# k by token from the DMA queue instead of TensorE in a fused linear-attention kernel, with state copies on GpSimd and other orders at both ends

## The reference, cut to what matters

```python
x = x + attn(layernorm(x), W_attn, b_attn, W_proj, b_proj)
x = x + ffn(layernorm(x), weight, bias)

# attn: 16 heads of 32; q, k = elu(.) + 1; v as it is
kv   = kv + k_t (outer) v_t        # running state, over the tokens of a sequence
ksum = ksum + k_t
y_t  = (q_t @ kv) / (q_t @ ksum + 1e-6)
attn = y @ W_proj + b_proj

# ffn: x and weight clipped to +-448 and rounded to float8_e4m3fn
ffn  = fp8(x) @ fp8(weight).T + bias
```

## Time and profile before

| what | us |
|---|---|
| runs of the kernel before | 987.88, 989.68, 990.79 |
| time of the profiled execution | 989.57 |
| its span, first to last instruction | 987.8 |
| TensorE busy in it | 951.9 |
| ScalarE busy | 743.6 |
| VectorE busy | 703.1 |
| GpSimd busy | 503.9 |

### The profile page before, as it was taken

One profiled execution on the slowest core, in us unless ns is written; L12 is line 12 of the kernel. 1 busy time (PEld: TensorE's weight loads), 2 busy tenths in 40 slices (PEclk: granted clock), 3 DMA queues, 4 the chain that ended last, 5 costly groups with the idle time before them and its releaser, 6 DMA issues.

```text
span 987.8 us, 44710 instructions
## 1 busy us (share of the span) xinstructions
PE 951.9 (96%) x19698; PEld 521.7 (53%) x19760; DVE 703.1 (71%) x1395; ACT 743.6 (75%) x1423; POOL 503.9 (51%) x521
## 2 busy tenths in 40 slices
PE   5998999999999999999999999999999999999985
PEld 2454555555555555555555555555555555555552
DVE  6977777676676777668677677767667676765674
ACT  5776686877878688787868868687786868777763
POOL 5536656555555455464555555555545546432323
PEclk9999999999999999999999999999999999999998
DMA  8824454544454434434335345454354453422311
GB/s 267 127 35 83 77 99 72 83 93 73 83 92 85 86 77 93 74 81 95 76 83 93 72 79 97 72 83 93 83 79 86 92 79 77 84 45 56 57 35 48
DMA packets 185362, 82.58 MB, mean 84 GB/s; under 512 B 165841, under 2 KB 165841, under 8 KB 185169
## 3 DMA queue, kind: packets, MB, share of 16 engines
q1 hardware_dynamic: 185168, 79.73, 42.6%
HBM read 22.81 MB, written 16.78 MB: 40 GB/s over the span
## 4 chain that ended last, share of the span: by engine, by line
PE 92%; DVE 4%; issue 1%; ACT 1%; POOL 1%; DMA 0%; POOLq 0%
PE R L219 76%; PE S L219 13%; PE R L223 3%; DVE raw L641 1%; POOL st L868 1%; DVE st L602 1%; POOL xn L870 0%; DVE xs L687 0%; DVE xs L697 0%; DMA xs<-in_L_attn_x 0%; ACT raw L409 0%; DVE v L630 0%; DVE wpl L769 0%; ACT wl L428 0%; DVE st L604 0%
## 5 line engine op out<-in xcount | busy, mean ns | idle before, releaser
L219 PE MATMUL R<-xt,wh 128*128 128x512 f16 x1024 | 306.8, 382 | 3.0 <-ACT wh L409 2.4
L409 ACT ACTIVATE raw<-qk 64x512 f32<-64x512 f32 x256 | 160.8, 628 | 76.8 <-PE S L219 73.8
L618 DVE SCALAR_TENSOR_TENSOR qk<-qk,rel 128x512 f32<-128x512 f32 x128 | 98.0, 768 | 149.8 <-ACT rel L421 145.3
L899 POOL TENSOR_TENSOR yhl<-y,yhl 128x512 f16<-128x512 f32 x60 | 69.5, 1159 | 255.8 <-ACT yhl L409 255.8
L219 PE MATMUL R<-xt,wl 128*128 128x512 f16 x512 | 194.2, 380 | 0.0
L868 POOL TENSOR_TENSOR st<-st,half 128x1 f32<-128x1 f32 x128 | 74.8, 584 | 168.3 <-DVE st L607 166.9
L219 PE MATMUL R<-wh,xt 128*128 128x512 f16 x512 | 160.3, 379 | 0.0
L641 DVE TENSOR_TENSOR raw<-S,causal 64x1024 f32<-64x1024 f32 x128 | 155.9, 1218 | 0.9
L219 PEld LDWEIGHTS R<-xt,wh 128*128 128x128 f16 x1024 | 96.8, 98 | 110.7 <-DVE xt L735 2.6
L418 ACT ACTIVATE qk<-R,bqk,wm 128x512 f32<-128x512 f32 x128 | 98.9, 772 | 61.4 <-PE R L219 61.3
L219 PE MATMUL R<-wph,yt 128*128 128x512 f16 x512 | 134.2, 385 | 2.0 <-DVE yt L680 2.0
(11 more groups left out here) (88 smaller groups left out, 1330.0 us busy)
## 6 DMA issues: line engine op xcount, KB each, us to landing
xs<-in_L_attn_x SPq DMA_DIRECT2D x64, 256.0 KB, 3.7
out<-xs SPq DMA_DIRECT2D x64, 256.0 KB, 2.3
raw<-in_L_attn_W_attn SPq DMA_DIRECT2D x3, 1024.0 KB, 10.6
xs<-in_L_attn_W_proj SPq DMA_DIRECT2D x4, 256.0 KB
raw<-in_L_ffn_weight SPq DMA_DIRECT2D x1, 1024.0 KB, 17.6
x2t<-x2b SPq DMA_TRANSPOSE x62, 2.4
xt<-xnhl SPq DMA_TRANSPOSE x60, 4.1
yt<-yhl SPq DMA_TRANSPOSE x60, 3.3
```

Of the source, the lines that this page charges most:

```text
L219: return e.matmul(out, a, b, start=start, stop=stop, skip_group_check=True)
L409: return e.activation(out, in_, ACT.Copy, **more)
L618: e.scalar_tensor_tensor(qk[j % 2][:, i, :], qk[j % 2][:, i, :], 1.0, rel[:, (u - 1) % 2, :], ALU.min, ALU.add).then_inc(s_phi, 1)
```

## The change

- k by token for tiles 1 to 63 no longer comes from TensorE. GpSimd (`k_split`) copies the low and the high 16-bit words of the tile's k apart (two copies, 512 words for each partition), the SP queue (`t_k`) transposes them into `kt`, and ScalarE copies the words back together into `ktok` (two copies in place of one). Tile 0 stays as it was. `khl` and `kt` lie in `raw`, where the second layer's weight is prepared first.
- Of the eight copies of `spread`, ScalarE drops the two of `mid` for the first two head groups; one GpSimd multiplication by a 0/1 table `pair` writes both (`spread` on GpSimd). `values(n)` on TensorE and `update` on VectorE wait for it (`s_near`).
- ScalarE's `ln1_parts(n + 8)` moves behind the third chunk.
- VectorE: `proj` is cut in `proj` and `ln2`. Where n + 1 is 60 to 63, `ln2(n - 1)` and `ffn(n - 2)` wait until stage n + 1, behind `scores(n + 1)`. `t_y(63)` goes ahead of `ln2`. In the opening, `proj_weight`, `ffn_high`, `ffn_round` and `ffn_sum` change places.
- TensorE's `proj` of a tail tile waits for the low half of y only before its ninth matmul.

```diff
@@ tensor
+                pe.wait_ge(s_near, n + 1)
...
                 if tail(n):
                     pe.wait_ge(s_yth, n - NT + 5)
-                    pe.wait_ge(s_ytl, n - NT + 5)
...
+                    if tail(n) and i == 8:
+                        pe.wait_ge(s_ytl, n - NT + 5)
...
-                    if n + 1 < NT:
-                        k_tokens(n + 1)
@@ scalar
-                act.wait_ge(s_ktr, n + 1)
+                dst = ktok[:, n % 2, :]
+                if n == 0:
...
+                act.wait_ge(s_kt[n % 2], 16 * ((n + 1) // 2))
                 if n >= 2:
                     act.wait_ge(s_delta, n - 1)
-                copy(ktok[:, n % 2, :], bank["ktok", n][:, :]).then_inc(s_ktok, 1)
+                words = dst.bitcast(I16).rearrange("p (d w) -> p w d", w=2)
+                for w in range(2):
+                    made = copy(words[:, w, :], kt[:, n % 2, 4 * w:4 * w + 4, :].rearrange("p g d -> p (g d)"))
+                made.then_inc(s_ktok, 1)
...
-                    for h in range(4):
+                    for h in range(2 * a, 4):
...
-                    if n + 8 < NT:
-                        ln1_parts(n + 8)
                     if n:
                         ahead(chunks(n)[1])
+                        if n + 8 < NT:
+                            ln1_parts(n + 8)
@@ vector
+                dve.wait_ge(s_near, n)
...
+            def ln2(n):
                 dve.wait_ge(s_x1, n + 1)
...
+                    if tail(n):
+                        ln2(n - 2)
+                        ffn(n - 3)
                     if n + 8 < NT:
                         ln1(n + 8)
                     if n == 0:
-                        ffn_high()
+                        proj_weight()
+                    if n == 1:
+                        ffn_sum(0, 2)
...
                     values(n)
                     if n == 0:
+                        ffn_high()
+                        ffn_round()
                         ahead(chunks(n)[1])
                 if 1 <= n <= NT:
                     proj(n - 1)
+                if n == NT - 1:
+                    t_y(n)
+                if 1 <= n <= NT and not NT - 4 <= n + 1 < NT:
+                    ln2(n - 1)
                 if n + 1 < NT:
                     update(n + 1)
-                if n == 0:
-                    proj_weight()
-                    ffn_round()
...
-                if n >= 2:
+                if n >= 2 and not NT - 4 <= n + 1 < NT:
                     ffn(n - 2)
@@ gpsimd
+            def spread(n):
...
+                pool.wait_ge(s_mid, n + 1)
+                held = mid[0:HALF, :].rearrange("p (g w) -> p g w", g=4).unsqueeze(2).broadcast_to([HALF, 4, 2, W])
+                rows = pair[:, :].unsqueeze(1).unsqueeze(3).broadcast_to([HALF, 4, 2, W])
+                e.tensor_tensor(v[0:HALF, 1, :, 0:2, :], held, rows, ALU.mult).then_inc(s_near, 1)
+
+            def k_split(n):
+                src, v, j, c = parts(n)
+                for g in range(4):
+                    pool.wait_ge(s_phi, phi_count(j, 4 + g))
+                if n >= 3:
+                    pool.wait_ge(s_kt[n % 2], 16 * ((n - 1) // 2))
+                words = src[:, 4:8, c * P:(c + 1) * P].bitcast(I16).rearrange("p g (t w) -> p w g t", w=2)
+                for w in range(2):
+                    made = e.tensor_copy(khl[:, n % 2, w, :].rearrange("p (g t) -> p g t", g=4), words[:, w, :, :])
+                made.then_inc(s_khl, 1)
...
             for n in range(NT + 1):
                 if n < NT:
                     if n + 8 < NT:
                         ln1(n + 8)
                     if n + 8 < NT:
                         add_bp(n + 8)
-                        ln1_parts(n + 8)
                     if n < 8:
                         add_bp(n)
+                    if n + 2 < NT:
+                        k_split(n + 2)
+                    if n + 8 < NT:
+                        ln1_parts(n + 8)
                     values(n)
                 if n >= 1:
                     proj(n - 1)
+                if n + 1 < NT:
+                    spread(n + 1)
@@ sync
+            def t_k(n):
+                sp.wait_ge(s_khl, n)
+                if n >= 3:
+                    sp.wait_ge(s_ktok, n - 1)
+                e.dma_start(kt[:, n % 2, :, :], khl[:, n % 2, :, :].rearrange("p a n -> p (a n)"),
+                            transpose=True).then_inc(s_kt[n % 2], 16)
...
                 if n >= 2:
                     t2(n - 2)
+                if n + 2 < NT:
+                    t_k(n + 2)
                 if n + 8 < NT:
                     t1(n + 8)
```

More of the change, by code:

```diff
@@ L13 @@
 I32 = mybir.dt.int32
+I16 = mybir.dt.int16
 D = 512
@@ L122, in build @@
         half = sb("half", [P, 1], F32)
+        pair = sb("pair", [HALF, 2], F32)
         st1 = sb("st1", [P, 4, 12], F32)
@@ L143, in build @@
         sm = raw[:, 2, :, :].rearrange("p h (a m) -> p h a m", a=2)
+        khl = raw[:, 0, 0:2, :].rearrange("p a n -> p (a n)").bitcast(I16).rearrange("p (i w n) -> p i w n", i=2, w=2)
+        kt = raw[:, 0, 2:4, :].rearrange("p a n -> p (a n)").bitcast(I16).rearrange("p (i k n) -> p i k n", i=2, k=8)
         w_b = raw[:, 1, 2:4, :].rearrange("p a n -> p (a n)").bitcast(BF16).rearrange("p (k n) -> p k n", k=4)
@@ L153, in build @@
         s_yt = [sem(f"yt{i}") for i in range(2)]
+        s_kt = [sem(f"kt{i}") for i in range(2)]
         s_x2t = [sem(f"x2t{i}") for i in range(2)]
@@ L171, in build @@
         s_rs1, s_xn, s_rs2, s_x2, s_xb, s_x1b = sem("rs1"), sem("xn"), sem("rs2"), sem("x2"), sem("xb"), sem("x1b")
-        s_yl, s_blank, s_one = sem("yl"), sem("blank"), sem("one")
+        s_yl, s_blank, s_one, s_khl, s_near = sem("yl"), sem("blank"), sem("one"), sem("khl"), sem("near")
         bank = {}
@@ L272, in proj_qkv, with k_tokens @@
                 mm.then_inc(s_qkv, 1)
[L274 to L277, removed]
+            def k_tokens():
+                out = take("ktok", s_ktok, 1)
                 for g in range(4):
-                    pe.wait_ge(s_phi, phi_count(j, 4 + g))
-                transposes(out, [src[:, 4 + g, cols] for g in range(4)]).then_inc(s_ktr, 1)
+                    pe.wait_ge(s_phi, phi_count(0, 4 + g))
+                transposes(out, [qk[0][:, 4 + g, 0:P] for g in range(4)]).then_inc(s_ktr, 1)
             def update(n):
@@ L377, in _ @@
                 if i == 9:
-                    k_tokens(0)
+                    k_tokens()
             update(0)
@@ L457, in k_tokens @@
             def k_tokens(n):
-                act.wait_ge(s_ktr, n + 1)
+                dst = ktok[:, n % 2, :]
+                if n == 0:
+                    act.wait_ge(s_ktr, 1)
+                    copy(dst, bank["ktok"][:, :]).then_inc(s_ktok, 1)
+                    return
+                act.wait_ge(s_kt[n % 2], 16 * ((n + 1) // 2))
                 if n >= 2:
                     act.wait_ge(s_delta, n - 1)
-                copy(ktok[:, n % 2, :], bank["ktok", n][:, :]).then_inc(s_ktok, 1)
+                words = dst.bitcast(I16).rearrange("p (d w) -> p w d", w=2)
+                for w in range(2):
+                    made = copy(words[:, w, :], kt[:, n % 2, 4 * w:4 * w + 4, :].rearrange("p g d -> p (g d)"))
+                made.then_inc(s_ktok, 1)
             def queries(n):
@@ L690, in proj @@
                     dve.wait_ge(s_x2, n - 3)
-                stats(x, st2[:, n % 4, :], s_bn2, s_var2, n)
+                stats(xs[:, n % NX, :], st2[:, n % 4, :], s_bn2, s_var2, n)
             def ffn(n):
@@ L791, in ffn_sum @@
                     e.tensor_tensor(w_b[:, f, :], w_hi[:, f, :], w_lo[:, f, :], ALU.add).then_inc(s_wfd, 1)
+            e.memset(pair[:, :], 0.0).then_inc(s_pair, 1)
+            dve.wait_ge(s_pair, 1)
+            for h in range(2):
+                e.memset(pair[32 * h:32 * h + 32, h:h + 1], 1.0).then_inc(s_pair, 1)
             no_state()
@@ L838, in _ @@
                     if n == 0:
-                        ffn_high()
-                    ahead(chunks(n)[0][:1])
-                    ahead(chunks(n)[0][1:])
+                        proj_weight()
+                    if n == 1:
+                        ffn_sum(0, 2)
+                    ahead(chunks(n)[0])
                     if tail(n - 1):
@@ L850, in _ @@
                     proj(n - 1)
+                if n == NT - 1:
+                    t_y(n)
+                if 1 <= n <= NT and not NT - 4 <= n + 1 < NT:
+                    ln2(n - 1)
                 if n + 1 < NT:
                     update(n + 1)
-                if n == 0:
-                    proj_weight()
-                    ffn_round()
                 if n == 1:
                     ffn_sum(2, 4)
-                if n == NT - 1:
-                    t_y(n)
-                if n >= 2:
+                if n >= 2 and not NT - 4 <= n + 1 < NT:
                     ffn(n - 2)
@@ L879, in ln1 @@
                 norm(xn[:, m % 2, :], xs[:, m % NX, :], st1[:, m % 4, :], s_rs1, s_xn, m)
+            def spread(n):
```

(12 more changed lines are left out.)

6 lines of the change are left out of this document (2 added, 4 removed).

## The result

The changed kernel took 985.95 us (median of 10 runs, 984.11 to 988.17), the kernel before, in the same rounds, 988.85 (10 runs). The ratio is 0.9972, 95% interval 0.9959 to 0.9986: faster, by 2.9 us where 12.5 were forecast. The profiled execution of the changed kernel is the fastest of its ten, 984.11 us, 5.46 under the profiled one of before.

What follows compares the result with a forecast made beforehand. TensorE, busy 96% of the span, was taken as the bound. Middle -25.5, opening -4 and last tiles +17 sum to -12.5, so 989.57 becomes 977; the likeliest case's range is 970 to 984, the whole range 960 to 988.

Steps and rivals of the forecast that it cites:

- (c): Opening: TensorE's stops before `values(1)` and `scores(2)` go, 5.1 us, less 1 given back; -4, bounds 0 and -5.5.
- (a): Middle tiles: k's transposes leave TensorE, 0.44 us each tile over 58 stages, 25.5 us off.
- (b): Middle tiles: new work on ScalarE, GpSimd and DMA is covered, `t1` lands in time; nothing is added.
- (d): Last tiles: postponed statistics hold up GpSimd's `spread`, loss 18.2; very end gains 1.4; together +17, bounds +12 and +24.
- I give back 1 us for that: Opening: allowance for y of tile 0 coming late by DMA, behind `k_split(2)` on GpSimd and `t_k(2)`, `t1(8)` queued.
- R1: Rival for the last tiles: their stall does not come, they gain about 3 us; 957, chance 0.12.
- the 1.3 us of slack of `t1`: Fourth tile of a block: `t1` issued at about 518.5 lands at 521.7, 1.3 us in time for the next block.
- R2: Rival at block starts: slow GpSimd copies make the fourth tile's `t1` late; +31, so 1008, chance 0.08.
- R3: Rival in the middle: ScalarE becomes the bound, at 1.26 us for each joining copy; 986.5, chance 0.08.
- R4: Rival in the middle: the DMA queue becomes the bound, tiles last 14.63 or more; 1002, chance 0.02.

Runs made afterwards that it cites:

- the last kernel: Changed kernel without postponement, x ahead of k, bias additions late in tiles 0 and 1, plus last two weight transposes behind tile 1's y: 957.37 us, ratio 0.9683.
- the first best version: Changed kernel without the postponement, with x's low half and transpose ahead of k's, and bias additions late in tiles 0 and 1: 959.29 us, ratio 0.9687.

## Why the prediction was wrong in size

The forecast was 977.0; the profiled execution is 7.1 above it, the median another 1.8. By the prediction's own steps:

| step | forecast | measured | off by |
|---|---|---|---|
| opening, to scores(3): (c), and one beat of (a) | -4.4 | -1.1 | +3.4 |
| middle, scores(3) to scores(59): (a), (b) | -25.1 | -22.7 | +2.4 |
| tail and end: (d) | +17 | +18.3 | +1.3 |

The forecast of the middle holds 0.44 for stage 59, which begins at `scores(59)`; without it, it is off by 1.9.

**The step that failed is (c)**, and in it the sentence "I give back 1 us for that", with a smaller failure in (b) below. TensorE's two old stops (for VectorE's mask before `values(1)`, and for y before `scores(2)`) went, as reckoned, but the wait for y of tile 0 took 4.21 us and the halved clock behind it another 2.2: projection and update lasted 5.6 us from 77.07 to 82.67 where the version with the bias additions late takes 3.45 (73.21 to 76.66). The give-back was a guess where a sum could have been made, as the one for `t1` in (b) was. GpSimd's list between xn and the low half of y is five operations, four of which took longer while VectorE worked on the weights: the bias additions 2.28 each instead of 1.28, the splits 1.3 each instead of 0.58. Undisturbed, y's low half would have been there an estimated 3.5 us earlier (2 x 1.0 + 1.47); and with GpSimd earlier the wait came one tile later, behind the weight transposes, as the experiment showed. A gain of the size forecast was seen only in the last kernel, with GpSimd's list and the queue both in order: its `scores(3)` starts 4.3 us before the old one.

**(d) was right in mechanism and size** (19.8 us against 18.2 for the stall, -1.6 against -1.4 from the last projection but one to the last). The chain behind the mask is the one written down; the chain in time of stage 60 of the changed kernel reads

```profile
906.15 1.23 DVE raw L656
...
907.41 0.71 DVE st L617
...
908.65 0.94 POOL st L893
...
910.69 1.07 issue
911.76 0.63 POOL v L916
...
912.52 1.99 PE S L226 x128
```

Two sizes in it were off and cancelled. The multiplication takes 0.63 and not 1.3 (it handles 264 elements for each partition, not 528). And the clock fell to half after every stop: 0.50 from 912 to 915 and 0.52 to 918, so that the projection behind it took 4.4 us (914.51 to 918.93) where 3.49 were reckoned. **But the price of R1 was wrong.** It took GpSimd's order for the only obstacle and put 957 on its removal; the run gave 978.6, since ScalarE and SP hold the same trap, and with all three removed 970.5. The postponement has a cost in every order tried.

**(a)** held: 14.19 a tile. **(b)** held in that ScalarE, GpSimd and DMA stayed covered (76%, 66%, q1 50.3%). ScalarE's copy into every second 16-bit word takes 0.77 and not 0.63, GpSimd's splits 0.72 in the mean and not 0.80; no wait of TensorE in the middle is put down to either. What failed in it is the 1.3 us of slack of `t1`: three times x came late, by 0.49, 0.37 and 1.16 us, though both splits together took 1.16 or 1.17 each time. In tiles 0 to 7 GpSimd does a second bias addition ahead of them, 2.51 us for two, which the sum, read from a tile behind these, left out; the first two waits come behind these. The longest is of the queue, as its chain shows:

```profile
843.85 1.18 POOL raw L926 x2
...
845.04 2.09 SPq L1046
...
847.23 4.66 DMA xt<-xnhl
```

The issue of k's transpose took 2.09 where 1.23 were reckoned, and x's landed 4.66 us after its own where 3.2 were taken from one row; the page of the kernel before has 4.1 as the median of all sixty. So R2's effect came, at a fifteenth of its price, but not its mechanism: GpSimd's splits were not slow. R3 and R4 did not come: the transposes of k land 3.4 us after their issue, in the median. The Trainium skill, "VectorE: DVE Perf Modes", section "The three transpose paths", would have had R4, as would the rule on 128x128 transposes in its section "Rules for kernel authors"; no wait for k's transpose is among those of TensorE and ScalarE.

## What to carry over

Postponing work on one engine postpones everything that stands behind its results in the order of the other engines and queues. List, for each engine and queue, the first instruction that will wait for the postponed result and what stands behind it, before taking the price of one such place for the price of all. A stop that is removed at one tile can be worth nothing, as here, until the same queue has been followed through the next tile. And where an engine gets new work, price its whole list up to the instruction that is waited for, in the stretch where it happens, not with the means of the middle.

## What the runs showed of the hardware

**A long VectorE operation on SBUF can hold up GpSimd.** The one-column power takes 0.55 us in the median. In the opening of the changed kernel it took 2.59, beside a VectorE operation of 2.34 that began just before:

```profile
57.20 2.34 DVE L787 SCALAR_TENSOR_TENSOR wpl<-xs,wm,wph 128x2048 f16<-128x2048 f32 x1
...
57.36 2.59 POOL L893 TENSOR_TENSOR st<-st,half 128x1 f32<-128x1 f32 x1 [4.33 <-DVE st L622]
```

It ended 0.4 us after VectorE's did, which fits a hold until VectorE's end better than a general slowdown. VectorE may be held too: its phi has a mean of 869 ns with the splits on GpSimd and 768 before, at a median of 693 in both. The Trainium skill, "SBUF — State Buffer", section "Terms", says that the two engines share a port pair by an exclusive lock, held for the full instruction, and that the loser blocks; the row of the power agrees. A long operation does not always hold for its whole length: beside two of VectorE of 3.02 and 2.18 us (61.88 to 67.11), GpSimd's two bias additions took 4.56 us instead of 2.56.

**A short stop of TensorE halves the clock behind it in some executions and not in others.** Behind 1.89 us in the kernel before it fell to 0.50 and behind 1.98 with the new opening alone it did not (1.00); behind 2.47 us with the bias additions late it fell, behind 2.30 in the first best version it did not. It is so between executions of one kernel too: those of the kernel before fall in two groups by their mean granted clock (0.992 to 0.994, and 0.989 to 0.991), with medians 2.7 us apart. Two kernels with the same stops can so differ by 1 to 3 us that belong to no edit.
